# Decoder layer on one Trainium2 core: the first layer's constants are issued behind the fusion's constants and the first block of W2

## Chip, cores and metric

One core of one Trainium2 chip. The metric is the device time of one execution in microseconds, the median of several runs. The time before is 1419.36 us (three runs: 1419.16, 1419.36 and 2244.75).

## What is computed

One pre-norm decoder layer over x [16, 512, 256] float32. There are three residual blocks: a Nystrom self-attention with 16 heads, 64 landmarks and six steps of a pseudo-inverse, a cross attention on a context of 64 rows, and a feed-forward block in which each batch item takes one of eight experts.

```python
x = x + attn(layernorm(x), Wqkv, bqkv, Wout, bout)
x = x + xattn(layernorm(x), ctx, ctx, mask, Wq, bq, Wk, bk, Wv, bv, Wo, bo)
x = x + ffn(layernorm(x), Wp1, bp1, Wp2, bp2, W1, b1, W2, b2, Wo, bo)
# in ffn, with sel the expert of the item and hs the normalised x:
h = gelu(hs @ W1[sel] + b1[sel])
out = (h @ W2[sel] + b2[sel]) @ Wo + bo
return hs + 0.3 * out
```

The product W2[e] @ Wo does not depend on x. The kernel works it out once for all eight experts at its start; this is called the fusion below.

## The kernel before

Five engines run one program each: S (SyncE, which issues the loads), P (TensorE), A (ScalarE), D (VectorE) and G (GpSimd). The order of the work is written out by hand as a list of steps. FIRST (line 61) has the start, TURN a steady turn that interleaves four batch items, LAST the end. A word such as `P.k.0@1` is the step k.0 of TensorE for batch item 1. Each engine runs its own steps in the order in which the list has them, and waits on semaphores for those of the others.

The steps at the start on which the change and the prediction bear:

- S.x@0 loads x of item 0 (512 KB, tile x_in), and behind it, in the same step, the four FIRST_CONSTS: Wqkv (768 KB), bqkv (3 KB), bv and bout (128 KB each). They count on one semaphore, first_consts_loaded.
- S.w2.e loads the transposed W2 of expert e (512 KB) into space that is free at the start: w2.2 into w1e, w2.3 into w2e, w2.1 and w2.0 into halves of hT, w2.7 into xnT_c, w2.5 into base, w2.6 into xn_c, w2.4 into x2. Each has a semaphore of its own.
- S.fc loads the three FUSE_CONSTS: the output weights wfo (256 KB), b2T and bfo_row (8 KB each), on the semaphore fuse_consts_loaded.
- P.f.e is the fusion of expert e, 16 matmuls in the trace, from wfo and the space of S.w2.e. The first one, P.f.2, waits for fuse_consts_loaded, w2.2 and pool_consts (small masks that GpSimd builds). P.f.1 and P.f.3 follow, and then the transposes P.xnTa.1@0 and P.xnTa.0@0 of the normalised x.
- D.lnA@0 (L1013, L1016) takes the statistics of x. D.nmA@0 waits for first_consts_loaded, makes four small constants (L1031 to L1037) and writes the normalised x into xn_a (L1042), which P.xnTa@0 reads.
- G.xr@0 (L685) adds bout to x, and so waits for first_consts_loaded. Behind it on GpSimd is G.cst@0 (L701 to L722), constants for later steps, and then G.kbd@0 (L681).
- P.k.0@0 and the other projections use Wqkv and also wait for first_consts_loaded.
- S.x@1, the load of the next x, waits for D.nmA@0 and G.xr@0. S.w2.0, S.w2.4, the rest of the constants (S.cn) and the context stand behind it on SyncE.

Of the kernel before, what the change touches and what calls it, by code (L numbers as in the profile page):

```python
# [13 lines left out]
P = 128  # L14
# [44 lines left out]


FIRST = """
    S.x@0 S.w2.2@0 D.lnA@0 S.fc@0 P.f.2@0 S.w2.3@0 S.w2.1@0 P.f.1@0 P.f.3@0 G.lnA@0 D.nmA@0 A.f.2@0
    P.xnTa.1@0 P.xnTa.0@0 S.w2.7@0 A.f.3@0 G.xr@0 S.w2.5@0 P.fb@0 A.xnTa.1@0 A.xnTa.0@0 P.k.0@0 P.q.1@0
    A.k.0@0 A.f.1@0 S.w2.6@0 P.k.1@0 D.lmk.0@0 P.q.0@0 P.f.7@0 A.k.1@0 S.x@1 G.cst@0 D.lmk.1@0 A.q.0@0
    A.q.1@0 D.fb@0 P.f.6@0 A.f.7@0 A.f.6@0 G.kbd@0 D.lnA@1 D.lmq.0@0 P.s1.1@0 P.s1.0@0 D.mx1.1.0@0
# [280 lines left out]
def decoder_kernel(nc, a, out):  # L346
    B, S, D = a["x"].shape
# [8 lines left out]
    with ExitStack() as ctx:  # L356
# [3 lines left out]
        def sem(name):  # L360
            return ctx.enter_context(nc.semaphore(name))
# [112 lines left out]
        first_consts_loaded = sem("first_consts_loaded")  # L474
# [14 lines left out]
        def first(eng, sem_, n):  # L489

            if passed.get((eng, sem_), 0) >= n:
                return False
            passed[eng, sem_] = n
            return True

        def unmet(eng, who, i, *steps):

            n = max(DONE[who, i, s] for s in steps) if i >= 0 else 0
            return n if first(eng, done[who], n) else 0
# [24 lines left out]
        def fused_space(e):  # L524

            return (hT[:, 0:2].rearrange("p a b -> p (a b)"), hT[:, 2:4].rearrange("p a b -> p (a b)"),
                    w1e[:].rearrange("p a b -> p (a b)"), w2e[:].rearrange("p a b -> p (a b)"),
                    x2[:].rearrange("p a b -> p (a b)"), base[:].rearrange("p a b -> p (a b)"),
                    xn["c"][:].rearrange("p a b -> p (a b)"), xnT["c"][:].rearrange("p a b -> p (a b)"))[e]
# [8 lines left out]
        def halves(w):  # L538
            return w.rearrange("(k p) n -> p k n", p=P)

        FIRST_CONSTS = [(wqkv[:], halves(a["Wqkv"])), (bqkv_col[:], a["bqkv"]), (bv_row[:], a["bv"]),
                        (bout_row[:], a["bout"])]
# [23 lines left out]
        @block.sync  # L566
        def _(sp):
            def body(i, step):
                kind = step[0]
                if kind == "x":  # L570
                    if c := unmet(sp, "D", i - 1, ("nmA",) if i == 1 else ("lnA",)):
                        sp.wait_ge(dve_done, c)
                    if c := unmet(sp, "G", i - 1, ("lnA",), ("xr",)):
                        sp.wait_ge(pool_done, c)
                    sp.dma_start(x_in[:], x_dram[:, i * T:(i + 1) * T, :]).then_inc(x_loaded, 16)
                    if i == 0:
                        for dst, src in FIRST_CONSTS:
                            sp.dma_start(dst, src).then_inc(first_consts_loaded, 16)
                elif kind == "fc":
                    for dst, src in FUSE_CONSTS:  # L580
                        sp.dma_start(dst, src).then_inc(fuse_consts_loaded, 16)
                elif kind == "cn":
                    for dst, src in CONSTS:
                        sp.dma_start(dst, src).then_inc(consts_loaded, 16)
                elif kind == "w2":
                    e = step[1]
                    sp.dma_start(fused_space(e).rearrange("p (k f) -> p k f", k=KD),
                                 w2T_dram[:, e * KD:(e + 1) * KD, :]).then_inc(w2_loaded[e], 16)
                elif kind == "ctx":
                    if c := unmet(sp, "P", i - 1, ("vx",)):  # L590
                        sp.wait_ge(pe_done, c)
                    sp.dma_start(ctxT[:], ctx_dram[:, :, i * LM:(i + 1) * LM]).then_inc(ctx_loaded, 16)
                elif kind == "f":
                    e = step[1]
                    if c := unmet(sp, "A", 0, step):
                        sp.wait_ge(act_done, c)
                    sp.dma_start(w2o_dram[e * P:(e + 1) * P, :], fused_space(e)).then_inc(fused_stored, 16)
                elif kind == "fb":
                    if c := unmet(sp, "D", 0, step):
                        sp.wait_ge(dve_done, c)  # L600
                    sp.dma_start(row_dram, bfo3_row[:]).then_inc(fused_stored, 16)
                elif kind == "ew1":
                    if c := unmet(sp, "D", i, ("logit",)):
                        sp.wait_ge(dve_done, c)
                    if c := unmet(sp, "P", i - 1, *[("h", n) for n in range(FM)]):
                        sp.wait_ge(pe_done, c)
                    if c := unmet(sp, "A", i - 1, *[("h", n) for n in range(FM)]):
                        sp.wait_ge(act_done, c)
                    if first(sp, fused_stored, 16 * FUSED):
                        sp.wait_ge(fused_stored, 16 * FUSED)  # L610
                    e = sp.value_load(sel8[0:1, 0:1], min_val=0, max_val=EXPERTS - 1)
                    sp.dma_start(w1e[:], w1_dram[:, bass.ds(e * KD, KD), :]).then_inc(expert_in_loaded, 16)
                    sp.dma_start(b1e[:], a["b1"][:, bass.ds(e * FM, FM)]).then_inc(expert_in_loaded, 16)
                elif kind == "ew2":
                    if c := unmet(sp, "D", i, ("logit",)):
                        sp.wait_ge(dve_done, c)
                    if c := unmet(sp, "P", i - 1, ("y3", 0), ("y3", 1)):
                        sp.wait_ge(pe_done, c)
                    if c := unmet(sp, "G", i - 1, ("row",)):
                        sp.wait_ge(pool_done, c)  # L620
                    if first(sp, fused_stored, 16 * FUSED):
                        sp.wait_ge(fused_stored, 16 * FUSED)
                    e = sp.value_load(sel8[0:1, 0:1], min_val=0, max_val=EXPERTS - 1)
                    sp.dma_start(w2e[:].rearrange("p k d -> p (k d)"),
                                 w2o_dram[bass.ds(e * P, P), :]).then_inc(expert_out_loaded, 16)
                    sp.dma_start(row_e[:],
                                 row_dram[bass.ds(e, 1), :].broadcast_to([P, D])).then_inc(expert_out_loaded, 16)

            for engine, i, step in PROGRAM:
                if engine == "S":  # L630
                    body(i, step)
            sp.wait_ge(stored, 32 * B)
# [1032 lines left out]
```

## Time and profile before

| | before |
|---|---|
| median of the runs | 1419.36 us |
| the profiled execution's own time | 1421.52 us |
| its span, first to last instruction | 1419.8 us |
| TensorE busy | 1369.3 us (96%) |
| VectorE busy | 1032.9 us (73%) |
| ScalarE busy | 666.6 us (47%) |
| GpSimd busy | 569.9 us (40%) |
| mean DMA rate over the span | 37 GB/s |
| DMA rate in the first fortieth of the span (35.5 us) | 281 GB/s |

The profile is of one execution. An engine's busy share is an average over stages, so a stage is read by its own rows: a timeline (start, duration, engine, line, operation, with the idle time ahead of it and what ended it in brackets), the chain of work that ended last, the DMA issues with the time from issue to landing, and busy time by stretches. Lines are those of the kernel before. "SPq" is SyncE's queue of DMA issues.

### The profile page before, as it was taken

What the parts mean: (1) busy time and instruction counts of PE and PEld (TensorE: products, weight loads), DVE (VectorE), ACT (ScalarE), POOL (GpSimd) and SP (SyncE); (2) the same over time, 40 slices, a digit from 0 to 9 for tenths busy, and PEclk for the clock granted to TensorE, in tenths of its full rate; (3) what the DMA queues carried; (4) which work ended last, traced back from release to release, by engine and by line L of the source; (5) the groups of instructions that cost most, each with busy time, mean ns of one, the idle gap of its engine ahead of it and who ended that gap; (6) DMA issues with size and microseconds to landing.
All of it is one profiled execution on the core that took longest, in us unless ns stands there. A gap on an engine that the chain in (4) does not pass through costs nothing.

```text
span 1419.8 us, 53827 instructions
## 1 busy us (share of the span) xinstructions
PE 1369.3 (96%) x23732; PEld 896.7 (63%) x23732; DVE 1032.9 (73%) x2194; ACT 666.6 (47%) x1230; POOL 569.9 (40%) x799
## 2 busy tenths in 40 slices
PE   6998999999999999999999999999999999999998
PEld 4756656655666666666666656666675656566555
DVE  2487877848677786867778686777878776898661
ACT  2423355354454545445454545545455453535652
POOL 6223444443615335361533526143352531516223
PEclk9999999999999999999999999999999999999999
DMA  8002010110101001010100101010010100001032
GB/s 281 1 3 91 5 62 3 44 66 11 57 12 51 19 30 39 3 57 12 50 19 19 51 3 57 12 51 18 15 55 4 51 3 19 18 4 37 3 97 64
DMA packets 40538, 53.19 MB, mean 37 GB/s; under 512 B 9699, under 2 KB 30451, under 8 KB 40307
## 3 DMA queue, kind: packets, MB, share of 16 engines
q1 hardware_dynamic: 31602, 41.37, 9.2%
q10 hardware_dynamic: 8704, 8.39, 1.7%
q8 instruction: 188, 3.08, 0.9%
q14 instruction: 44, 0.35, 0.1%
HBM read 37.16 MB, written 12.59 MB: 35 GB/s over the span
## 4 chain that ended last, share of the span: by engine, by line
PE 89%; DVE 4%; issue 2%; ACT 2%; DMA 1%; POOL 1%; DVEq 0%; SPq 0%; POOLq 0%; ACTq 0%
PE bank L1312 41%; PE bank L1555 8%; PE bank L1321 7%; PE bank L1331 7%; PE bank L1542 4%; PE bank L1381 2%; PE bank L1510 2%; PE bank L1446 2%; PE bank L1402 2%; PE bank L1435 2%; PE bank L1523 2%; PE bank L1369 1%; PE bank L1461 1%; PE bank L1408 1%; PE bank L1544 1%
## 5 line engine op out<-in xcount | busy, mean ns | idle before, releaser
L768 POOL TENSOR_TENSOR b<-ut,eye 128x256 f32<-128x256 f32 x192 | 137.2, 730 | 517.2 <-DVE ut L1151 445.2
L930 ACT ACTIVATE az<-bank 128x320 f32<-128x320 f32 x192 | 67.5, 400 | 191.6 <-PE bank L1321 191.2
L1208 DVE RECIPROCAL oT_x<-bank 128x256 f32<-128x256 f32 x64 | 109.3, 1734 | 22.5 <-PE bank L1555 22.5
L1312 PE MATMUL bank<-xnT_a,wqkv 128*128 128x512 f32 x256 | 123.6, 609 | 0.3 <-ACT xnT_a L854 0.3
L1312 PE MATMUL bank<-xnT_c,w1e 128*128 128x512 f32 x256 | 118.7, 605 | 3.0 <-DMA b1e<-in_b 3.0
L1208 DVE RECIPROCAL oT<-bank 128x256 f32<-128x256 f32 x64 | 111.5, 1747 | 10.4 <-PE bank L1555 10.3
L1312 PE MATMUL bank<-w2e,hT 128*128 128x256 f32 x512 | 117.3, 383 | 0.9 <-ACT hT L996 0.9
L1080 DVE TENSOR_REDUCE m<-bank 128x1 f32<-128x512 f32 x128 | 82.9, 680 | 39.4 <-PE bank L1402 37.9
L886 ACT ACTIVATE p3T<-bank 128x512 f32<-128x512 f32 x128 | 66.7, 604 | 83.4 <-PE bank L1435 83.4
L1312 PEld LDWEIGHTS bank<-w2e,hT 128*128 128x128 f32 x512 | 94.9, 190 | 15.2 <-issue 1.7
L1142 DVE SCALAR_TENSOR_TENSOR wb<-bank,eye 128x256 f32<-128x256 f32 x192 | 73.2, 411 | 33.0 <-PE bank L1321 32.3
L949 ACT ACTIVATE pT_x<-bank,neg_bias 128x512 f32<-128x512 f32 x128 | 79.8, 695 | 32.9 <-PE bank L1544 32.8
L1182 DVE TENSOR_REDUCE m<-bank 128x8 f32<-128x512 f32 x128 | 81.8, 682 | 16.2 <-PE bank L1510 16.0
L1182 DVE TENSOR_REDUCE m_x<-bank 128x8 f32<-128x512 f32 x128 | 79.5, 681 | 14.4 <-PE bank L1523 14.2
L1160 DVE SCALAR_TENSOR_TENSOR uz<-uz,bank 128x320 f32<-128x320 f32 x192 | 78.5, 436 | 8.9 <-PE bank L1331 5.8
L1331 PEld LDWEIGHTS bank<-wb,az 64*64 64x64 f32 x2560 | 46.3, 134 | 59.0 <-ACT az L930 20.9
L996 ACT ACTIVATE hT<-bank,b1e 128x512 f32<-128x512 f32 x64 | 43.3, 683 | 80.6 <-PE bank L1312 80.3
L1312 PEld LDWEIGHTS bank<-xnT_c,w1e 128*128 128x128 f32 x256 | 47.4, 192 | 52.0 <-issue 45.4
L1321 PEld LDWEIGHTS bank<-uz,ut 64*64 64x64 f32 x3072 | 60.5, 133 | 29.2 <-DVE uz L1160 18.2
L948 ACT ACTIVATE pT<-bank 128x512 f32<-128x512 f32 x128 | 68.5, 604 | 18.2 <-PE bank L1544 18.2
L1151 DVE SCALAR_TENSOR_TENSOR ut<-ut,bank 128x256 f32<-128x256 f32 x160 | 61.5, 408 | 19.4 <-PE bank L1331 18.4
L1321 PE MATMUL bank<-uz,ut 64*64 64x80 f32 (+1 forms) x3072 | 73.1, 229 | 2.5 <-issue 1.2
(223 smaller groups left out, 3005.0 us busy)
## 6 DMA issues: line engine op xcount, KB each, us to landing
x_in<-in_x SPq DMA_DIRECT2D x16, 512.0 KB, 3.9
w1e<-in_W SPq DMA_DIRECT2D x16, 512.0 KB, 3.6
w2e<-w2o SPq DMA_DIRECT2D x16, 512.0 KB, 4.0
out<-base ACTq DMA_DIRECT2D x32, 256.0 KB, 2.2
row_e<-w2o_row SPq DMA_DIRECT2D x16, 128.0 KB, 4.5
hT<-in_W2T SPq DMA_DIRECT2D x2, 512.0 KB, 6.5
pT_x<-in_ctxT SPq DMA_DIRECT2D x1, 1024.0 KB
ctxT<-in_ctxT SPq DMA_DIRECT2D x16, 64.0 KB, 2.4
```

Of the source, the lines that this page charges most:

```text
L768: return g.tensor_tensor(b7[:, q, :], ut[:, q, :], eye[28 if it else 7][:].unsqueeze(1) .broadcast_to([P, 4, LM]), ALU.subtract).then_inc( ...
L948: return s.activation(pT[x][:, 4 * k + j, :], src, ACT.Exp).then_inc(act_done, 1)
L949: return s.activation(pT[x][:, 4 * k + j, :], src, ACT.Exp, bias=neg_bias[:, i:i + 1]).then_inc(act_done, 1)
L1080: return v.tensor_reduce(m3[:, k, j:j + 1], tile(i, ("s3", k), j)[:], AX.X, ALU.max).then_inc(dve_done, 1)
L1142: return v.scalar_tensor_tensor(wb[:, h], src, 1.0 / 16 if it else 1.0, eye[15][:].unsqueeze(1).broadcast_to([P, 4, LM]), ALU.mult, ALU.ad ...
L1160: return v.scalar_tensor_tensor(uz[:, q, lo:], uz[:, q, lo:], 3.25 if it else 13.0, src[:, :, lo:], ALU.mult, ALU.subtract).then_inc(dve_d ...
L1182: return v.tensor_reduce(m[x][:, :, j, 2 * k:2 * k + 2], tile(i, ("s" + x, k), j)[:].rearrange("p (t h c) -> p t h c", t=T, h=2), AX.X, AL ...
L1208: return v.reciprocal(oT[x][:, k, cols], tile(i, ("den" + x, k))[:, cols]).then_inc(dve_done, 1)
L1312: last = mm(dst, lhsT, rhs, start=(k == 0), stop=(k == len(pairs) - 1))
L1321: last = mm(tile(i, step, r)[64 * c:64 * c + 64, w * j + lo:w * j + hi], lhsT[q, j + 4 * c, 0:LM], rhs[q, j + 4 * c, lo:hi], start=True, s ...
L1331: last = mm(tile(i, step, c)[64 * r:64 * r + 64, w * j + lo:w * j + hi], lhsT[q, r, j, 0:LM], rhs[q, r, j, lo:hi], start=True, stop=True)
L1555: last = mm(o[rows(j), :], w, pT[x][:, 4 * n + j, :], start=True, stop=True)
```

## The change

The four loads of FIRST_CONSTS leave the step S.x@0 and become a step of their own, S.qc@0. In the list, S.fc@0 moves directly behind S.x@0, and S.qc@0 stands behind S.w2.2@0 and D.lnA@0. Nothing else differs: the same loads, sizes, tiles and semaphores, and the same compute steps.

```diff
 FIRST = """
-    S.x@0 S.w2.2@0 D.lnA@0 S.fc@0 P.f.2@0 S.w2.3@0 S.w2.1@0 P.f.1@0 P.f.3@0 G.lnA@0 D.nmA@0 A.f.2@0
+    S.x@0 S.fc@0 S.w2.2@0 D.lnA@0 S.qc@0 P.f.2@0 S.w2.3@0 S.w2.1@0 P.f.1@0 P.f.3@0 G.lnA@0 D.nmA@0 A.f.2@0
...
                     sp.dma_start(x_in[:], x_dram[:, i * T:(i + 1) * T, :]).then_inc(x_loaded, 16)
-                    if i == 0:
-                        for dst, src in FIRST_CONSTS:
-                            sp.dma_start(dst, src).then_inc(first_consts_loaded, 16)
+                elif kind == "qc":
+                    for dst, src in FIRST_CONSTS:
+                        sp.dma_start(dst, src).then_inc(first_consts_loaded, 16)
```

Of the five engines, SyncE alone has its instructions in another order. This is the start of its program, as a difference between before (-) and the change (+). L578 and L581 are the issues of FIRST_CONSTS (L578 in before and change alike) and of FUSE_CONSTS; `w1e<-in_W2T` is S.w2.2, `w2e<-in_W2T` S.w2.3, `hT<-in_W2T` S.w2.1.

```order
 L575 DMA x_in<-in_x 128x4x256
+L581 DMA wfo<-in_Wfo 128x2x256
+L581 DMA b2T<-in_b2T 128x16
+L581 DMA bfo_row<-in_bfo 8x256
+L587 DMA w1e<-in_W2T 128x2x512
 L578 DMA wqkv<-in_Wqkv 128x2x768
 L578 DMA bqkv_col<-in_bqkv 128x6
 L578 DMA bv_row<-in_bv 128x256
 L578 DMA bout_row<-in_bout 128x256
-L587 DMA w1e<-in_W2T 128x2x512
-L581 DMA wfo<-in_Wfo 128x2x256
-L581 DMA b2T<-in_b2T 128x16
-L581 DMA bfo_row<-in_bfo 8x256
 L587 DMA w2e<-in_W2T 128x2x512
 L587 DMA hT<-in_W2T 128x2x512
```

Three fusion constants and the first block of W2 stand ahead of Wqkv and its biases instead of behind them; from w2e on, the queue is as it was.

TensorE's program starts with these rows in both kernels, with the semaphores that each waits for.

```order
L1312 MATMUL bank<-wfo,w1e 128x256 [waits w2_loaded2,fuse_consts_loaded,pool_consts]
L1312 MATMUL bank<-wfo,w1e 128x256 x7
L1312 MATMUL bank<-wfo,hT 128x256 [waits w2_loaded1]
L1312 MATMUL bank<-wfo,hT 128x256 x7
L1312 MATMUL bank<-wfo,w2e 128x256 [waits w2_loaded3]
L1312 MATMUL bank<-wfo,w2e 128x256 x7
L1369 MATMUL bank<-ident,xn_a 128x128 [waits dve_steps_done]
L1369 MATMUL bank<-ident,xn_a 128x128 x7
```

No row moved here; the loads for which the first row waits are those that stand further ahead on SyncE now.

VectorE's program starts with these rows in both kernels.

```order
L1013 BN_STATS stats_a<-x_in 128x6 [waits x_loaded]
L1013 BN_STATS stats_a<-x_in 128x6 x3
L1016 BN_AGGR mv_a<-stats_a 128x2 x4
L1031 TENSOR_SCALAR bq_col<-bqkv_col 128x2 [waits pool_consts,first_consts_loaded]
L1032 TENSOR_REDUCE par_qk<-head_mask 128x2
L1033 TENSOR_REDUCE quad<-head_mask 128x4
L1035 TENSOR_SCALAR par_mean<-par_qk 128x2
L1037 TENSOR_SCALAR par_qk<-par_qk 128x2
L1042 TENSOR_SCALAR xn_a<-x_in,mv_a,rstd_first 128x256 [waits pool_steps_done]
```

No row moved here either; the load for which L1031 waits stands further behind on SyncE now.

## Rows read from the trace of the kernel before

**Rows 1.** The page's fourth part: the chain that ended last, by engine.

```profile
PE 89%; DVE 4%; issue 2%; ACT 2%; DMA 1%; POOL 1%; DVEq 0%; SPq 0%; POOLq 0%; ACTq 0%
```

**Rows 2.** The same chain in order of time from 0 (start us, us, what).

```profile
5.06 5.40 DMA bfo_row<-in_bfo
...
10.55 13.54 PE bank L1312 x48
```

**Rows 3.** SyncE's issues, timeline from 0 (start, us, queue, line, operation, out<-in).

```profile
0.81 0.45 SPq L575 DMA_DIRECT2D x_in<-in_x  x1
1.31 0.50 SPq L578 DMA_DIRECT2D wqkv<-in_Wqkv  x1
...
2.83 0.43 SPq L578 DMA_DIRECT2D bout_row<-in_bout  x1
3.31 0.65 SPq L587 DMA_DIRECT2D w1e<-in_W2T  x1
4.00 0.47 SPq L581 DMA_DIRECT2D wfo<-in_Wfo  x1
...
5.56 0.39 SPq L587 DMA_DIRECT2D w2e<-in_W2T  x1
5.99 0.47 SPq L587 DMA_DIRECT2D hT<-in_W2T  x1
...
13.12 0.37 SPq L575 DMA_DIRECT2D x_in<-in_x  x1
```

**Rows 4.** DMA issues by stretches of the start: size, us from issue to landing.

```profile
x_in<-in_x SPq DMA_DIRECT2D x1, 512.0 KB, 4.4
...
bout_row<-in_bout SPq DMA_DIRECT2D x1, 128.0 KB, 5.1
...
w1e<-in_W2T SPq DMA_DIRECT2D x1, 512.0 KB, 6.0
...
hT<-in_W2T SPq DMA_DIRECT2D x1, 512.0 KB, 6.9
```

**Rows 5.** Busy time by stretches; the last two numbers are DMA share and GB/s.

```profile
0.00:5.00 5.00, 0.00 (x0) 0.00 (x0) 0.00 (x0) 1.28 (x1) 3.23 (x18) 1.00 0.53 168
5.00:10.00 5.00, 0.00 (x0) 0.00 (x0) 3.37 (x14) 0.00 (x0) 2.83 (x6) 1.00 1.05 358
```

**Rows 6.** VectorE, timeline of the start.

```profile
7.97 0.17 DVE L1031 TENSOR_SCALAR bq_col<-bqkv_col 128x2 f32<-128x2 f32 x1 [0.89 <-DMA bout_row<-in_bout]
...
9.05 4.04 DVE L1042 TENSOR_SCALAR xn_a<-x_in,mv_a,rstd_first 128x256 f32<-128x256 f32 x4 [0.28 <-POOL rstd_first L696]
...
32.41 0.69 DVE L1063 TENSOR_REDUCE ksum<-kT 128x64 f32<-128x512 f32 x1 [2.75 <-ACT kT L874]
...
33.71 1.39 DVE L1013 BATCH_NORM_STATS2 stats_a<-x_in 128x6 f32<-128x256 f32 x4
```

**Rows 7.** GpSimd, timeline of the start.

```profile
8.97 2.34 POOL L685 TENSOR_TENSOR xr<-x_in,bout_row 128x1024 f32<-128x1024 f32 x1
...
27.24 0.31 POOL L722 MEMSET vx_bd<- 128x256 f32 x1
33.18 0.76 POOL L681 TENSOR_TENSOR kbd<-ksum,par_mean 128x128 f32<-128x128 f32 x2 [5.63 <-DVE ksum L1063]
```

**Rows 8.** TensorE, timeline of the start.

```profile
10.55 6.62 PE L1312 MATMUL bank<-wfo,w1e 128*128 128x256 f32 x16 [10.55 <-DMA bfo_row<-in_bfo]
17.01 3.62 PE L1312 MATMUL bank<-wfo,hT 128*128 128x256 f32 x16
...
23.92 1.04 PE L1369 MATMUL bank<-ident,xn_a 128*128 128x128 f32 x8
...
40.20 1.17 PE L1510 MATMUL bank<-kbd,qT 32*128 32x128 f32 x32
...
44.48 3.62 PE L1312 MATMUL bank<-wfo,hT 128*128 128x256 f32 x16
```

**Rows 9.** The tile wfo: its matmuls by partner, ns min/median/max, first and last start.

```profile
L1312 PE MATMUL bank<-wfo,w1e x16: 379/634/767, 10.6 to 16.8; 128*128 128x256 f32 x16
L1312 PE MATMUL bank<-wfo,w2e x16: 378/379/380, 20.5 to 23.7; 128*128 128x256 f32 x16
```

## Prediction, made before the changed kernel was run

> **What bounds the kernel now.** I read first the chain that ended last. TensorE makes up 89% of it [rows 1], so what counts is when TensorE starts and where it stands still. I then read the beginning of that chain: before TensorE there is only SyncE and one DMA, the landing of bfo_row, issued at 5.06 us and landed 5.40 us later, at 10.46. TensorE starts at 10.55, and the chain stays on it for the next 13.5 us [rows 2]. For these 10.55 us TensorE does nothing, and no other row of the chain can cover them. The question is how much earlier the first matmul starts, and whether TensorE can keep that lead through the steps that follow.
>
> Third, SyncE's issues [rows 3] and their landings [rows 4]. The first matmul needs x's neighbours wfo, b2T, bfo_row and w2.2 (tile w1e). Ahead of the last of them the queue now holds x, Wqkv, bqkv, bv and bout. In the stretches the DMA engines move 168 GB/s from 0 to 5 us and 358 GB/s from 5 to 10, at a busy share of 1.05 [rows 5]: they are full from the moment that data flows, so bytes that stand ahead in the queue cost time.
>
> **The change, part by part.** Issue: each of the first issues takes about 0.5 us of SyncE. x is issued at 0.81 and the next at 1.31. The three fusion constants took from 4.00 to 5.56, 1.56 us [rows 3], so w2.2 is issued at 1.31 + 1.56 = 2.87, against 3.31 before, and bfo_row just ahead of it instead of at 5.06. The nine issues between x and w2e are the same nine, so w2e, hT and all later ones up to the second x keep their times from 5.56 on.
>
> Bytes: by 5.0 us 168 x 5 = 840 kB have moved. Up to and with w2.2 the queue now holds 524 (x) + 262 (wfo) + 8 + 8 + 524 = 1326 kB, so its last byte moves at 5.0 + 486/358 = 6.4 us. Landing comes after the last byte by a lag, which I take from loads of before in the same way. bout ends 1576 kB, by this count at 7.06, and landed at 2.83 + 5.1 = 7.93: 0.9. w2.2 ends 2100 kB, 8.52, and landed at 9.31: 0.8. bfo_row ends 2378 kB, 9.30, landed 10.46: 1.2. hT ends 3427 kB, 12.2, landed 5.99 + 6.9 = 12.89: 0.7 [rows 2 to 5]. With lags of 0.7 to 1.2 w2.2 lands between 7.1 and 7.6. The other lower bound is x, which had nothing ahead of it and took 4.4 us [rows 4]: 2.87 + 4.4 = 7.27. I take 7.4, and TensorE starts 0.09 later (10.55 against 10.46), at 7.5. **The gain at the first matmul is 10.55 - 7.5 = 3.05 us.**
>
> Does TensorE keep it? The steps behind it, each with what is late next:
>
> - P.f.2 took 10.55 to 17.01, 6.46 us [rows 8], and would end at 13.96. P.f.1 needs hT, which lands at 12.89 as before. Cover 1.1 us, cost nothing.
> - Wqkv and its biases now end the same 2378 kB that bfo_row ended, so they land at about 10.46 instead of 7.93. D.nmA waits for them (L1031 started at 7.97, rows 6). From L1031 to the end of L1042 it is 1.08 + 4.04 us, so xn_a is written by 10.5 + 5.1 = 15.6 us, not 13.1. P.xnTa needs it at 23.92 - 3.05 = 20.9 [rows 8]. Cover 5.2 us, cost nothing. The later Wqkv matmuls stand behind that.
> - On GpSimd xr moves from 8.97 to 10.5 and everything behind it by the same 1.5 us: the last constant ends at 27.55 + 1.5 = 29.1, and kbd needs ksum, 33.10 - 3.05 = 30.05 [rows 6, 7]. Cover 1.0 us. Without it kbd would be late by the rest, but its reader, the s1 matmuls, stands at 40.20 - 3.05 = 37.15 [rows 8], another 6 us off. Cost nothing.
> - On SyncE the second x waits for D.nmA: at most 13.12 + 2.5 = 15.6 us. Behind it stand w2.0, w2.4, the other constants and the context, all later by the same 2.5 us or less. VectorE reads the second x at 33.71 [rows 6], and w2.0 is read by P.f.0 at 44.48 [rows 8]. Both have more than 10 us. Cost nothing.
>
> From then on every row waits on TensorE or on work that TensorE releases, so the whole schedule should move as one piece. Nothing is done less, so no more than this start can be won. **Sum: 1421.52 - 3.05 = 1418.47 us** for the profiled execution. The median of the runs lies 2.16 us below that execution (1419.36), so the predicted median is 1419.36 - 3.05 = **1416.3 us**, 0.2%.
>
> **Rivals.**
>
> *The landing is a matter of latency, not of bytes.* If a load needs the same time from its issue, w2.2 takes its 6.0 us again [rows 4]: 2.87 + 6.0 = 8.87, start 8.96, gain 1.6, time 1417.8 us. For it speaks that all landings lie within 4.4 to 6.9 us of the issue; against it, that this time grows down the queue while the rate stays at 358 GB/s. Chance 0.15. The Trainium skill, "DMA: Bandwidth & Descriptors", section "Anatomy of one DMA", names a fixed cost of about 2.0 us beside the bytes at 436 GB/s; by it a lone w2.2 would land at about 6.1 us, an estimate, and the median be 1415.0. The row of x (4.4 us with nothing ahead) does not agree, and goes before it.
>
> *The clock rises at another moment.* In the first step the matmuls take 634 ns at the median and 379 at the end, later ones 379 throughout [rows 9]. By these, and although the granted clock column shows 1.00 from 0 to 10 us [rows 5], the engine begins at the lower of its two levels (1.2 GHz) after its idle start and then stays at 2.4. P.f.2 pays 6.46 - 3.45 = 3.0 us for it. With TensorE starting earlier this stretch may be shorter; but P.f.1 can't start before hT lands at 12.89, so at most 13.96 - 12.98 = 1.0 us more is won: 1415.3 us. Chance 0.1. The Trainium skill, "TensorE: Matmul & The Clock Gate", Part 1, says that the number of matmuls at the lower clock differs from run to run of one kernel; one profile here can't show that.
>
> *The lead is given back* (no change, 1419.4 us). Some wait after the start would have to be for something that TensorE does not release. The only such things that I find are loads, and each has its cover above; later loads follow from steps. But the turns interleave four items with waits of tenths of a microsecond, and a shift can fall into any of them. Chance 0.15.
>
> *Slower, by the constants that were moved back.* D.nmA waits for all four of FIRST_CONSTS, and TensorE stands in order at P.xnTa. If they landed not at 10.5 but after 10.5 + 5.2 = 15.7, TensorE would wait; from 18.7 on the 3.05 us are lost and the kernel is slower, by as much as they come later: at 20 us it is 1420.7. For it: 786 kB of Wqkv share the engines with four further blocks of W2 issued within 3 us. Against it: loads landed in order of issue before, and hT, two blocks further down, landed at 12.89 [rows 3, 4]. Chance 0.03.
>
> **How the numbers follow.** Forecast 0.57, latency 0.15, lead given back 0.15, clock 0.1, slower 0.03. Runs of the same kernel differ by about 2.2 us (the profiled one against the median). The forecast's landing bounds of 7.1 to 8.9 us alone give 1415.9 to 1417.8. With the clock's 1.0 and the 2.2 of spread below, the low end is 1413.0; with no gain and some spread above, the high end is 1420.8. A measurement can tell about 2%, 28 us; the whole idle start is 10.55 us, so no case reaches that on either side. Faster by over 2%: 0.01; within 2%: 0.98; slower: 0.01.
>
> **What would show it.** In the profile of the changed kernel: w2.2 issued at 2.9 us and landed at 7.1 to 7.6; the first matmul at 7.5; P.f.1 following it without a gap near 14; L1031 at about 10.5 and the end of xn_a by 15.6; P.xnTa at 20.9 with no wait for VectorE; the s1 matmuls near 37.2; a span of about 1416.8. The prediction is wrong if the first matmul starts after 9 us, if TensorE waits for hT or xn_a, or if it has the lead at 40 us and not at the end.

## The result, and the profile after

The changed kernel's median is 1417.16 us (22 runs, 1415.3 to 1422.38), that of the kernel before, timed beside it, 1421.29 us (22 runs, 1417.69 to 1426.39 and one slow run of 2244.75, which the ratio leaves out). The ratio is 0.9977, with a 95% interval of 0.9967 to 0.9987: a gain of 3.3 us, between 1.8 and 4.7. The two medians alone lie 4.1 us apart. The forecast was 1416.3 us and a gain of 3.05. The profiled execution took a span of 1418.4 us against 1419.8.

The chain that ended last, of the changed kernel (start us, us, what), against [rows 2]:

```profile
2.78 6.36 DMA w1e<-in_W2T
9.14 0.14 issue
9.28 13.64 PE bank L1312 x48
```

The chain now starts at w2.2 (tile w1e), issued at 2.78 us as worked out (2.87). But it landed at 9.14, not at 7.4, and TensorE started at 9.28, not at 7.5. Of the lead of 3.05 us this execution has 1.27.

SyncE's issues in the timeline, against [rows 3]:

```profile
0.81 0.45 SPq L575 DMA_DIRECT2D x_in<-in_x  x1
1.31 0.50 SPq L581 DMA_DIRECT2D wfo<-in_Wfo  x1
...
2.78 0.39 SPq L587 DMA_DIRECT2D w1e<-in_W2T  x1
3.21 0.46 SPq L578 DMA_DIRECT2D wqkv<-in_Wqkv  x1
...
5.21 1.06 SPq L587 DMA_DIRECT2D w2e<-in_W2T  x1
6.32 0.93 SPq L587 DMA_DIRECT2D hT<-in_W2T  x1
```

The rows of w2.2 and of Wqkv, which is issued behind it (DMA issues by stretches; the last number is us from issue to landing), against [rows 4]:

```profile
w1e<-in_W2T SPq DMA_DIRECT2D x1, 512.0 KB, 6.4
...
wqkv<-in_Wqkv SPq DMA_DIRECT2D x1, 768.0 KB, 5.5
```

w2.2 has a semaphore of its own, and its row is its landing. The 5.5 us in the row of Wqkv are not: the four constants count on one semaphore, and the row tells only when the first 16 of its 64 counts had come. The trace also has every DMA packet with its size. Packets of 3 KB, one row of Wqkv each, are Wqkv's alone in the first 22 us. The last of its 256 ended at 10.64 us, but 243 of them, 746 kB, had ended when w2.2 landed at 9.14. The DMA rates by stretches, against [rows 5], are as before:

```profile
0.00:5.00 5.00, 0.00 (x0) 0.00 (x0) 0.24 (x1) 1.28 (x1) 3.23 (x18) 1.00 0.56 178
5.00:10.00 5.00, 0.72 (x2) 0.66 (x3) 1.55 (x8) 0.00 (x0) 1.86 (x5) 1.00 0.98 347
```

By 9.14 us 178 x 5 + 347 x 4.14 = 2327 kB had moved. Only 1326 kB end with w2.2; of the rest, some 1000 kB, nearly all belongs to the four constants behind it (1052 kB together), 746 kB to Wqkv by its packets.

TensorE's timeline, against [rows 8]:

```profile
9.28 6.71 PE L1312 MATMUL bank<-wfo,w1e 128*128 128x256 f32 x16 [9.28 <-DMA w1e<-in_W2T]
15.83 3.62 PE L1312 MATMUL bank<-wfo,hT 128*128 128x256 f32 x16
...
22.74 1.04 PE L1369 MATMUL bank<-ident,xn_a 128*128 128x128 f32 x8
...
39.03 1.17 PE L1510 MATMUL bank<-kbd,qT 32*128 32x128 f32 x32
```

From the first row on, each stands 1.2 us ahead of before, with no wait for a load or for VectorE. VectorE and GpSimd, against [rows 6, 7]:

```profile
11.91 0.17 DVE L1031 TENSOR_SCALAR bq_col<-bqkv_col 128x2 f32<-128x2 f32 x1 [5.29 <-DMA bout_row<-in_bout]
...
12.29 2.46 DVE L1035 TENSOR_SCALAR par_mean<-par_qk 128x2 f32<-128x2 f32 x1
...
15.07 1.70 DVE L1042 TENSOR_SCALAR xn_a<-x_in,mv_a,rstd_first 128x256 f32<-128x256 f32 x4
```

```profile
11.96 2.34 POOL L685 TENSOR_TENSOR xr<-x_in,bout_row 128x1024 f32<-128x1024 f32 x1 [3.41 <-DMA bout_row<-in_bout]
...
30.21 0.32 POOL L722 MEMSET vx_bd<- 128x256 f32 x1
32.00 0.76 POOL L681 TENSOR_TENSOR kbd<-ksum,par_mean 128x128 f32<-128x128 f32 x2 [1.48 <-DVE ksum L1063]
```

The moved constants landed at 11.9 us and not at 10.5, xn_a was written by 16.8 and not by 15.6, and GpSimd had its constants done at 30.5 and still waited 1.48 us for ksum. Both delays stay in their cover.

Two questions are left. Why did w2.2 land 1.7 us later than its bytes and lag say? And why is the timed gain, 3.3 us, larger than the lead of 1.27 us in the profiled execution?

### The profile page after: what moved, and what is told of

Same layout as the page of the kernel before. It is cut to its first block, busy times and chain, and to the rows that moved or that the text cites. A ratio compares the mean times of both kernels' runs of the same rounds, so it can differ in the third digit from the quotient of the medians.

```text
span 1418.4 us, 53827 instructions
## 1 busy us (share of the span) xinstructions
PE 1370.8 (97%) x23732; PEld 897.1 (63%) x23732; DVE 1032.7 (73%) x2194; ACT 667.1 (47%) x1230; POOL 571.0 (40%) x799
## 4 chain that ended last, share of the span: by engine, by line
PE 89%; DVE 4%; issue 2%; ACT 2%; DMA 1%; POOL 1%; DVEq 0%; POOLq 0%; SPq 0%; ACTq 0%
PE bank L1312 41%; PE bank L1555 8%; PE bank L1321 7%; PE bank L1331 7%; PE bank L1542 4%; PE bank L1510 2%; PE bank L1381 2%; PE bank L1446 2%; PE bank L1402 2%; PE bank L1435 2%; PE bank L1523 2%; PE bank L1369 1%; PE bank L1461 1%; PE bank L1408 1%; PE bank L1544 1%
```

## Experiments

Theory A: a load that is issued right behind w2.2 shares the DMA engines with it and delays it. Theory B: the small rows of b2T and bfo_row ahead of it delay it. Theory C: landings simply vary. For the time, the theory is that TensorE's lead at its start is carried to the end one for one, and the rival that the turns change it.

### The two kernels again

r_before and r_before2 are the kernel before, r_after, r_after2 and r_after3 the changed kernel, all unedited.

> The kernel before once more, unchanged, for how much its start differs between executions. Theory A (the start moves with the loads that share the queue, and is much the same each time): first matmul at 10.3 to 10.8 us, last load bfo_row. Theory C (the landings vary by a microsecond or more between executions, and the 9.28 us of the changed kernel was an unlucky one): first matmul anywhere between 9.5 and 11.5. In both, the span less the first matmul is 1409.3 us within 0.5, if the lead is kept to the end.

> The changed kernel once more, unchanged. Theory A: first matmul again at 9.1 to 9.5 us. Theory C: it differs by over 0.5 us, and can be at the 7.5 us that was forecast. The span less the first matmul is 1409.1 us within 0.5 if the lead is kept.

> The kernel before once more, unchanged. First matmul at 10.3 to 10.6 us as in the two profiles so far, and the steady turns at the same distance from it, but for steps where the granted clock differs.

> The changed kernel once more, unchanged, timed beside the one before. Expected: first matmul at 8.7 to 9.4 us, 1.1 to 1.8 us of lead over before, and the same lead at every step of the steady turns between 400 and 1100 us but for steps of 0.5 to 1.7 us at the places where the granted clock falls in one execution and not in the other. Median below before by the 1.1 to 1.8 us if the lead is all that the change does; by over 2 us with an interval that leaves 1.8 out if there is a second gain.

> The changed kernel a fourth time, for its profile: w2.2 somewhere between 7.6 and 9.2 us, Wqkv at about 9, and TensorE starting 0.1 us behind w2.2. If the landing of w2.2 is under 7.5 the spread is as wide as I take it, if all four lie above 7.5 the loads behind it always cost something.

Measured, with the profiles shown so far in the first row of each (landing of the last load that TensorE awaits at its start, first matmul, start of the s1 matmuls, span and the mean granted clock; us):

```
              last load         first matmul   s1      span     clock
before        bfo_row 10.46     10.55          40.20   1419.8   0.996
r_before      bfo_row 10.28     10.38          39.62   1422.0   0.994
r_before2     bfo_row 10.27     10.36          40.03   1419.8   0.995
after         w2.2     9.14      9.28          39.03   1418.4   0.994
r_after       w2.2     8.6       8.73          38.01   1413.9   0.997
r_after2      w2.2     7.6       7.74          36.77   1420.9   0.993
r_after3      w2.2     8.6       8.75          38.20   1423.8   0.992
```

Before starts within 0.2 us each time. The changed kernel's start lies between 7.74 and 9.28: the spread that theory C asks for, but only in this order of loads. The start of r_after, 8.73, lies below the 9.1 to 9.5 that theory A expected, and that of r_after2, 7.74, below the 8.7 to 9.4 expected then. The expectation for the span less the first matmul, 1409.3 and 1409.1 us within 0.5, failed too: it was 1411.6 in r_before and 1405.2 in r_after. So one profile of each kernel can't tell whether a lead of 1 or 2 us is kept; the section on the differences between runs takes this up. Its mean is 8.63 against 10.43, a lead of 1.8 us at the first matmul, and 38.0 against 39.95, of 1.95 us, at s1. The forecast start of 7.5 was nearly met once. In that execution the next load came into play, as the timeline of r_after2 shows:

```profile
7.74 5.39 PE L1312 MATMUL bank<-wfo,w1e 128*128 128x256 f32 x16 [7.74 <-DMA w1e<-in_W2T]
13.47 3.72 PE L1312 MATMUL bank<-wfo,hT 128*128 128x256 f32 x16 [0.34 <-DMA hT<-in_W2T]
```

The first step took 5.4 us instead of 6.5, because more of its matmuls ran at the upper clock (464 ns at the median against 634 in the first profile of the changed kernel, 379 at the end in both), and TensorE then waited for hT. r_after2, timed beside the kernel before, gave a ratio of 0.9985 (0.9972 to 0.9999): a gain of 2.1 us, which leaves the lead of 1.8 within the interval. The expectation of the same lead at every step between 400 and 1100 us did not quite hold: against the first profile of before it grows by 0.9 to 1.9 us between 640 and 1060 us, but so does that of r_before and r_before2 (1.4 and 0.9 us), so this lies in that one execution of before.

### A wait behind w2.2

hold is the changed kernel with

```diff
                 elif kind == "qc":
+                    sp.wait_ge(w2_loaded[2], 16)
                     for dst, src in FIRST_CONSTS:
```

and hold2 and hold3 are the same kernel again.

> The changed kernel with one wait more: SyncE issues the first layer's constants, and all that follows, only when w2.2 has landed. Theory A (w2.2 landed at 9.14 instead of 7.4 because the 1048 kB issued right behind it shared the DMA engines with it): w2.2 lands at 7.1 to 7.6 us and the first matmul starts at 7.2 to 7.7. Theory B (the 64-byte rows of b2T and the 8 rows of bfo_row ahead of it held it up): it lands at about 9.1 again. Time: f.1's block hT is issued some 2 to 4 us later than before and lands at 15 to 17, so up to 3 us of the lead are given back; the whole within 3 us of the changed kernel either way.

> The kernel with the wait for w2.2 ahead of the first layer's constants once more, unchanged, for its profile. The theory (what is issued right behind w2.2 delays it, by an amount that differs between executions) expects w2.2 to land again at 7.0 to 7.4 us, as in its first profile (7.19). The rival (landings simply vary by two microseconds from execution to execution, whatever stands behind) expects 7.2 to 9.2.

> The same a third time: again 7.0 to 7.4 us by the theory, anywhere from 7.2 to 9.2 by the rival. Three landings within 0.3 us against three of the changed kernel that spread over 1.6 us would speak for the theory.

The chains of hold, hold2 and hold3, one after the other:

```profile
2.79 4.41 DMA w1e<-in_W2T
9.56 6.45 DMA hT<-in_W2T
```

```profile
2.79 4.52 DMA w1e<-in_W2T
9.68 6.54 DMA hT<-in_W2T
```

```profile
2.78 4.83 DMA w1e<-in_W2T
9.98 6.32 DMA hT<-in_W2T
```

With the queue empty behind it, and the same small rows ahead, w2.2 lands at 7.20, 7.31 and 7.61 us, against 7.6 to 9.1 in the changed kernel. That is the forecast's 7.4. The third is 0.2 beyond the band expected for it, and the three lie 0.4 us apart, not 0.3. The mean difference is 1.1 us (7.37 against 8.5), but the two groups touch: the earliest landing of the changed kernel is 7.60. The landings alone would be thin evidence. The packets say more. These are w2.2's time from issue to landing, and how much of Wqkv had been moved when it landed:

```
               us    kB of Wqkv
hold          4.41     0
hold2         4.52     0
hold3         4.83     0
r_after2      4.81   347
r_after       5.81   632
r_after3      5.83   614
after         6.36   746
```

In hold all 1326 kB up to and with w2.2 had moved by then and nothing else. In the changed kernel the engines moved Wqkv's packets while w2.2 still had some to come. A load that is late for another reason would also leave time for them, so the table shows the sharing, and hold against the changed kernel shows its price, which in r_after2 was about nothing. That is theory A; theory B is not needed for it, and theory C holds for how much the loads behind take, which differs from execution to execution (why it does stays open). The wait in hold keeps back the blocks of W2 as well as the constants, so hold alone does not tell which of them matter. The kernel late, below, has blocks of W2 right behind w2.2 in place of the constants, and there w2.2 again took 5.8 us (2.79 to 8.60). The time is another matter. hT is issued at 9.6 instead of 6.3 and TensorE waits for it, as hold's timeline shows:

```profile
7.33 6.30 PE L1313 MATMUL bank<-wfo,w1e 128*128 128x256 f32 x16 [7.33 <-DMA w1e<-in_W2T]
16.06 5.37 PE L1313 MATMUL bank<-wfo,hT 128*128 128x256 f32 x16 [2.43 <-DMA hT<-in_W2T]
```

Its busy time by stretches (the column ahead of the last two is the granted clock):

```profile
14.00:16.00 2.00, 0.00 (x0) 0.00 (x0) 1.84 (x3) 0.75 (x2) 1.81 (x6) 1.00 1.03 395
16.00:18.00 2.00, 1.94 (x5) 1.58 (x6) 1.32 (x4) 0.00 (x0) 1.62 (x7) 0.51 1.06 410
18.00:20.00 2.00, 2.00 (x8) 1.65 (x7) 0.00 (x0) 0.00 (x0) 1.44 (x6) 0.64 0.86 236
```

TensorE stood still for 2.43 us, and then the granted clock was 0.51, the lower level, for 2 us; the step took 5.4 us instead of 3.6. In hold2 TensorE waited 2.82 us and the step took 6.7 us. The s1 matmuls stand at 41.01, 42.55 and 41.33 us, 1 to 2.6 later than before, and the ratio is 1.0007 (0.9989 to 1.0024). At s1 all of the lead and more is gone.

### The small constants out of the way

split loads wfo alone ahead of w2.2, on a semaphore of its own, and b2T and bfo_row behind the first layer's constants:

```diff
-    S.x@0 S.fc@0 S.w2.2@0 D.lnA@0 S.qc@0 P.f.2@0 ...
+    S.x@0 S.fc@0 S.w2.2@0 D.lnA@0 S.qc@0 S.fcb@0 P.f.2@0 ...
...
-        FUSE_CONSTS = [(wfo[:], halves(a["Wfo"])), (b2T[:], a["b2T"]), (bfo_row[:], a["bfo"])]
+        FUSE_CONSTS = [(b2T[:], a["b2T"]), (bfo_row[:], a["bfo"])]
...
                 elif kind == "fc":
+                    sp.dma_start(wfo[:], halves(a["Wfo"])).then_inc(wfo_loaded, 16)
+                elif kind == "fcb":
                     for dst, src in FUSE_CONSTS:
...
                 elif kind == "f":
-                    fuse_consts(pe)
+                    if first(pe, wfo_loaded, 16):
+                        pe.wait_ge(wfo_loaded, 16)
```

> The changed kernel with b2T and bfo_row, which no step of the first fusions reads, behind the first layer's constants, and wfo on a semaphore of its own. w2.2 is issued at 1.8 us instead of 2.8. Theory A (bytes issued behind it share): it lands at about 8.1 to 9.0 us, since Wqkv follows as closely as before; the gain over the changed kernel is the 1 us of issue or less. Theory B (the small rows ahead): it lands at 6.5 to 7.4 us and the first matmul starts 1.9 us or more before that of the changed kernel. Median 0.2 to 1 us (A) or 1.9 to 2.7 us (B) below the changed kernel.

The chain of split:

```profile
1.86 5.79 DMA w1e<-in_W2T
```

w2.2 is issued at 1.86 and lands at 7.65 us: 5.8 us after its issue, as in two of the four changed executions (5.8). By this one profile the 0.93 us of issue are won, and nothing is seen of a delay by the small rows themselves. The landing falls between the two expectations (8.1 or later, 7.4 or earlier), so this run alone doesn't decide between A and B. s1 stands at 37.30. The ratio is 0.9995 (0.9975 to 1.0014): at most 3.6 us gained, and the expected gain over the changed kernel can't be told from none.

### The order of need

wfirst2 takes split and puts wfo and w2.2 ahead of x, and w2.1 (hT) ahead of the constants. wfirst2b is the same again.

```diff
-    S.x@0 S.fc@0 S.w2.2@0 D.lnA@0 S.qc@0 S.fcb@0 P.f.2@0 S.w2.3@0 S.w2.1@0 P.f.1@0 ...
+    S.fc@0 S.w2.2@0 S.x@0 S.w2.1@0 D.lnA@0 S.qc@0 S.fcb@0 P.f.2@0 S.w2.3@0 P.f.1@0 ...
```

> The start in the order of need: wfo and w2.2 ahead even of x, then x, w2.1, the first layer's constants, b2T and bfo_row (wfo on a semaphore of its own), w2.3. The theory (what is issued right behind a load shares the engines with it, and TensorE's lead at the first matmul is carried to the end) expects w2.2, issued at 1.3 us, to land at 6.0 to 7.1, the first matmul at 6.1 to 7.2, no gap ahead of P.f.1 and P.f.3, xn_a written by 17 us and read at about 20: the s1 matmuls at 35.7 to 36.8 us and a median 2 to 3 us below the changed kernel and 3.3 to 4.5 below the one before. The rival (the lead is given back in the turns) expects the same start and the time of the changed kernel.

> The order of need once more, timed again: w2.2 landed at 6.31 us in its first profile and the median was 5.7 us below the one before. TensorE's lead at the s1 matmuls was 4.8 us, so the median should lie 4 to 5.5 us below the kernel before, and the interval should leave no change out. If it comes out at 3 us or less, the first timing was flattered by the clock.

The chain of wfirst2, and its TensorE timeline:

```profile
1.31 4.96 DMA w1e<-in_W2T
```

```profile
6.41 5.68 PE L1315 MATMUL bank<-wfo,w1e 128*128 128x256 f32 x16 [6.41 <-DMA w1e<-in_W2T]
11.93 3.62 PE L1315 MATMUL bank<-wfo,hT 128*128 128x256 f32 x16
...
35.12 1.17 PE L1513 MATMUL bank<-kbd,qT 32*128 32x128 f32 x32
```

First matmul at 6.41 us (6.29 in wfirst2b), s1 at 35.12 (35.45), a lead of 4.7 us over before, partly from an earlier rise of the clock in the first step (5.5 and 6.0 us until the next step starts, against 6.1 to 6.5 in before). Both s1 are ahead of the band expected, by 0.6 and 0.25 us, and the median of wfirst2 lies further below before (5.6 us) than the 3.3 to 4.5 expected. The ratios are 0.9958 (0.9945 to 0.9972) and 0.9971 (0.9952 to 0.9990): 6.0 and 4.1 us under before. The medians are 1416.33 and 1417.11 us, 5.6 and 2.3 us under those of before beside them. So by its median the second timing falls below the 3 us that was to say that the clock had flattered the first; by its ratio it lies within the 4 to 5.5 expected. In that second timing four of the 17 runs of before had a mean clock of 0.997 or more and took 1415.3 to 1417.4 us, and no run of wfirst2b was above 0.996. Beside wfirst2 the changed kernel had 1419.06. wfirst2 is the best version here: both intervals leave no change out, and the comparison at equal clock below gives 4.8 us.

### The constants too late

late puts S.w2.7, S.w2.5 and S.w2.6 ahead of S.qc@0 as well and makes S.qc wait for w2.6, the last of them. The three leave the two lines of FIRST below, which the cut does not show.

```diff
-    S.x@0 S.fc@0 S.w2.2@0 D.lnA@0 S.qc@0 P.f.2@0 S.w2.3@0 S.w2.1@0 P.f.1@0 P.f.3@0 G.lnA@0 D.nmA@0 A.f.2@0
+    S.x@0 S.fc@0 S.w2.2@0 D.lnA@0 P.f.2@0 S.w2.3@0 S.w2.1@0 P.f.1@0 P.f.3@0 S.w2.7@0 S.w2.5@0 S.w2.6@0 S.qc@0 G.lnA@0 D.nmA@0 A.f.2@0
...
                 elif kind == "qc":
+                    sp.wait_ge(w2_loaded[6], 16)
```

> The changed kernel with the first layer's constants issued only when the six blocks of W2 issued ahead of them have landed (about 17 us). For the rival in which the constants come too late: they land at about 21 us, L1031 starts there and xn_a is written 4.9 us later, at 26, where TensorE wants it at about 22.5. It should wait some 3 to 4 us ahead of P.xnTa, so that the s1 matmuls stand at 42 to 43.5 us, against 38.0 to 39.0 in the changed kernel. If the wait is shorter than 2 us, VectorE's part behind the landing was counted too long.

The chain of late, and the row in which TensorE waits:

```profile
16.45 3.79 DMA bout_row<-in_bout
...
23.05 1.49 DVE xn_a L1043 x4
```

```profile
24.58 1.64 PE L1370 MATMUL bank<-ident,xn_a 128*128 128x128 f32 x8 [2.29 <-DVE xn_a L1043]
```

```profile
24.00:26.00 2.00, 1.42 (x8) 1.25 (x8) 0.53 (x2) 0.59 (x1) 1.62 (x7) 0.74 0.08 15
26.00:28.00 2.00, 2.00 (x7) 0.41 (x5) 0.00 (x0) 0.60 (x2) 1.39 (x6) 0.50 0.88 296
```

The constants landed at 20.2 us (expected 21) and xn_a was written 4.3 us later (expected 4.9), so the wait is 2.3 us, under the 3 to 4 expected. TensorE's clock then fell to its lower level again (0.74 and 0.50 in the last two rows, by stretches), and s1 stands at 42.12 us, 2.2 behind before. The mechanism of the slower rival is real. Its price at s1 has two parts: P.xnTa stands 0.9 us behind before (24.58 against 23.67, the mean of the three profiles), and from there to s1 it is 17.5 us instead of 16.3.

## Where the runs differ

The gain of 2 to 3 us must be read out of runs of one kernel that lie up to 13 us apart (before, 1414.42 to 1427.31). The stretches show what makes most of that. Before at 138 us, then the changed kernel at 136 us:

```profile
138.00:140.00 2.00, 0.67 (x36) 0.60 (x36) 0.00 (x0) 1.57 (x4) 1.85 (x4) 1.00 1.04 422
140.00:142.00 2.00, 2.00 (x64) 1.14 (x64) 1.90 (x6) 0.64 (x2) 0.80 (x3) 1.00 0.95 370
```

```profile
136.00:138.00 2.00, 0.55 (x32) 0.56 (x32) 0.00 (x0) 1.67 (x5) 1.85 (x5) 1.00 1.03 420
138.00:140.00 2.00, 2.00 (x24) 0.56 (x13) 1.79 (x6) 0.00 (x0) 0.92 (x3) 0.57 0.95 371
140.00:142.00 2.00, 2.00 (x69) 1.64 (x64) 0.65 (x5) 1.53 (x4) 0.00 (x0) 0.58 0.17 49
```

In both TensorE waits some 1.4 us there in the same steps. In the changed kernel the granted clock then fell to 0.57 and in before it stayed at 1.00. Between 116 and 186 us the lead shrank from 1.42 to 0.24 us. In r_before and r_before2 the clock falls there too, in r_after2 it does not, so it is not a trait of either kernel. Other such places lie near 292, 1172 and 1392 us.

The mean granted clock of an execution thus goes with most of the difference. Over the 51 runs of before for which a clock is on record, the span falls by about 1.5 us for 0.001 of mean clock (correlation -0.93). Mean spans of runs with the same mean clock (us, number of runs):

```
clock     before          changed        difference
0.994     1421.6  (9)     1418.9  (5)    2.7
0.995     1419.6 (20)     1417.0 (10)    2.6
0.996     1417.7 (10)     1414.9 (12)    2.8
```

A fit of span against clock and kernel over all 124 runs gives, against before: changed -2.6 us (95% interval 0.5), hold -0.4 (0.8), split -2.7 (0.8), wfirst2 -4.8 (0.7). The leads at s1 were 1.95, -1.7, 2.65 and 4.7 us. For split and wfirst2 the lead at 40 us is the gain at the end. For the changed kernel 0.6 us are not accounted for; its start varies by 1.5 us and only four were seen, so this may be chance. For hold the fit is 2.1 us better than its lead, and here the comparison at equal clock misleads. hold's own wait lowers the clock: over the first 40 us the granted clock is 0.96, 0.91 and 0.96 in its three profiles and 1.00 in those of before and of the changed kernel. That alone lowers the mean of an execution by 0.0011 to 0.0025, an estimate from 40 us out of 1420, and at 1.5 us for 0.001 it is 1.7 to 3.8 us that the fit takes off hold's time. Without the clock hold's spans lie 0.9 us above those of before (95% interval 1.7), which leaves room for the 1.7 us lost at s1.

## Why the prediction was right or wrong

**What bounds it** was right. The change shortened the chain's idle start, and TensorE's share of the chain stayed at 89%.

**Issue times**: w2.2 at 2.78 against 2.87, right. w2e and what follows did not keep their times: its issue took 1.06 us and hT's 0.93 instead of 0.39 and 0.47, so hT was issued at 6.32, 0.3 us later. It landed at 14.54, not at 12.89 (13.4 to 14.0 in the other three): from issue to landing it took 8.2 us instead of 6.9, with the same bytes ahead of it. No run isolates why. The constants too landed late, at 11.9 and not at 10.5.

**Bytes and lag, landing at 7.1 to 7.6**: this is the step that failed. It counted only bytes that stand ahead of a load. The runs of hold show that it is right when nothing stands behind (7.20 to 7.61), and the changed kernel, with 1052 kB and then W2 right behind, landed w2.2 1.1 us later on average, up to 1.8 over hold's mean. In the kernel before there were loads behind too, and the lags of 0.7 to 1.2 us taken from it contain whatever those cost there. bfo_row, the load that counted there, is 8 KB at the end of a full queue, whose landing came at 10.27 to 10.46 each time. The gain at the first matmul was therefore 1.27 us in the profiled execution and 1.8 on average, and not 3.05.

**The covers** held: hT by 1.3 us (15.83 against 14.5), xn_a by 6 us (16.8 against 22.74), kbd by 1.5 us, and the second x, issued at 16.80 instead of by 15.6, by far. In r_after2 the cover of hT was gone, by 0.34 us, as the clock rival had said.

**One for one to the end** fits what was measured, but is not shown to a microsecond: the fit's 2.6 us (0.5) lies just above the lead of 1.95, and hold can't be used at equal clock. For the rest, late and wfirst2 moved s1 by +2.2 and -4.7 us and ended +2.2 (one run) and -4.8 by the fit at equal clock.

**The number** was near for a reason that is partly luck. 1416.3 was forecast from a lead that was 1.2 us too large, against a median of before of three runs (1419.36) that was 1.9 below the one found over 22. The gain at equal clock, 2.6 us, lies between the latency rival (1.6) and the forecast (3.05). The latency rival's landing of 8.87 is nearer to the four seen (mean 8.5), but its cause is not: w2.2 took 4.4 to 4.8 us from issue with an empty queue behind it, not 6.0. The sentence beside that rival on the fixed cost of 2.0 us needs two corrections. The Trainium skill, "DMA: Bandwidth & Descriptors", section "Anatomy of one DMA", fits that figure to DMAs issued by GpSimd, and this one is issued by SyncE; the 3.2 us that it gives for 512 KB are less than any row here, even those of hold. And by the prediction's own limit at hT (12.89) a start at 6.2 us gives 1415.3, not 1415.0.

**The slower rival** did not occur. late shows its mechanism with the constants landing at 20.2 us. The rival's rule gives 1.5 us slower for that; the wait alone made 0.9, because VectorE's part behind the landing was 4.3 us and not 5.1, and the lower clock added 1.3, which the rival did not have.

## What to carry to other kernels

At a start that waits for loads, issue them in the order in which they are needed, and count as part of a load's time not only the bytes ahead of it but also those issued right behind it. Holding those back helps the one load and starves the next, so the better cure is to put the next needed load behind it, as wfirst2 does. Where a change is worth 0.2%, take several profiles of each kernel and compare runs at equal granted clock, unless the change itself lowers the clock, as hold does.

## What the hardware showed that I had not expected

The packets of one queue do not move strictly in order of issue: Wqkv was issued 0.43 us behind w2.2, and 347 to 746 kB of it had moved when w2.2 landed. The Trainium skill, "DMA: Bandwidth & Descriptors", section "Queues, rings and completion order", says that completion is not first-in first-out per issuing engine. No run here shows a whole load overtaking another: the loads with a semaphore of their own landed in order of issue in all fourteen profiles. Where several loads share one semaphore, as the four constants do, the profile's time to landing is that of a count and not of the load it is printed beside (8.7 us for Wqkv, whose last packet ended at 10.64).

A wait of TensorE of 1.4 to 2.8 us can be followed by a lower clock that costs up to another 3.1 us (the step behind it in hold2, 6.71 against 3.62; 5.37 in hold), and in two executions with the same wait the clock falls in one and not in the other (0.57 against 1.00 near 138 us). Such falls go with most of the 13 us between runs of one kernel.

par_mean, a 128x2 operation of VectorE, took 2.46 us beside GpSimd's xr and 0.17 us in before, where it ran before xr. There the first copy into xn_a carried the stall instead (2.98 us of the 4.04 for four, against 1.70 for all four now). Moving the constants moved the stall and did not add one. The Trainium skill, "SBUF — State Buffer", section "Who interferes with whom", says that VectorE in its two-port mode and GpSimd lock each other out of a shared pair of ports for the whole instruction; these durations agree (the same operation took 2.04 us beside xr in late), though no run here took xr away.
